# A second score buffer, values eight slots later, and the weight scales spread over the first 20 slots

## The chip, the cores and the metric

The kernel runs on one core of a Trainium2 chip. The metric is the time of one execution on the device, in microseconds (us). The kernel before takes 847.64 us, the median of three runs (847.51 to 848.23).

## What is computed

The reference is one block of a transformer on x of 4 x 2048 x 256 in fp32: attention with one head of 256, then a gated feed-forward that mixes each row with the row before it, each with a layer norm before and behind it and a residual around it.

```
x = x + layernorm(attn(layernorm(x)))
    qkv = the columns 0:64 and 192:256 of x in fp16, 64:192 in fp32, times weight_qkv
    s = softmax((q / 16) k^T);  y = s v;  attn = y out_w^T + out_b
x = x + layernorm(ffn(layernorm(x)))
    xr = mu_r x + (1 - mu_r) x_prev;  xk = mu_k x + (1 - mu_k) x_prev
    ffn = sigmoid(xr W_r^T) * (relu(xk W_k^T)^2 W_v^T)
```

## The kernel before

The 4 x 2048 rows are cut into 32 steps of 256 rows (two tiles of 128; `RT` = 2, `H` = 32), and each step's keys into four blocks of 512. A step has so eight **units**, a tile against a block. Time is counted in **slots**: slot k computes the scores of unit k, and every other stage of a step h stands at slot 8h plus an offset from a table of numbers. All engines run through the same slots, each with its own list of what it does in one; nothing else sets the order. Within a step the stages are: scores (TensorE, 5 matmuls of 512 columns into one of three PSUM banks S), a copy to the fp32 buffer `probs` with the running maximum (VectorE, `score_out`), `row_bias` behind the last block of a tile, the exponential (ScalarE, `exponents`, in place in `probs`), its upper fp16 half `p_hi` (ScalarE, `probs_high`) and the rest `p_lo` (VectorE, `probs_low`), four transposing DMAs from SyncE's queue, the values (TensorE, `attend`, 10 matmuls of 256 columns in each of eight slots), the projection, the norms and the feed-forward (`project_out`, `attention`, `turn_mix_in`, `mix`, `receptance`, `mix_keys`, `feed`, `gated`, and small norms on GpSimd). fp32 products are made of fp16 halves, three or five matmuls to a product.

In a step's first 16 slots stand `EXP` (4, 8), `HIGH` (6, 9), `LOWER` (7, 10), `TURN_P` (7, 11) for its two tiles, and `VALUES` 15: the scores of step h are in slots 8h to 8h+7, its values in 8h+15 to 8h+22. `probs` has one set of two tiles, so that the first copy of a tile waits for `p_lo` of the same tile one step earlier (line 792). The first step takes its units in another order (tile by tile in turn) and has its own offsets, `FIRST_EXP` and the like.

Ahead of the slots the kernel folds the query and key weights into one matrix, norms the first 2048 rows, splits them into fp16 halves (`planes_high` on ScalarE, `planes_low` on VectorE) and turns them by DMA. The other weights are scaled by powers taken from their peaks: `turn_weight` and `multiply_weights` in slot 2, `peaks_of` in 4, a turn of the peaks in 6, `diagonal_of_peaks` in 8, its spread and `tops` in 9, `scales` on GpSimd, `weight_high` in 11 and 13, `weight_low` in 12 and 14. The rows of batches 1 to 3 are prepared in the slots of the batch before, by four groups of stages from `PREP` on, 12 slots apart.

## Time and profile before

| | |
|---|---|
| median of three runs | 847.64 us |
| the profiled execution | 845.67 us |
| its span, first to last instruction | 843.9 us |
| TensorE busy | 796.9 us, 94% of the span |
| VectorE busy | 704.0 us, 83% |
| ScalarE busy | 516.9 us, 61% |
| GpSimd busy | 420.9 us, 50% |
| DMA | 101.59 MB, mean 120 GB/s |

The page of the profile cuts the span into 40 slices of 21.1 us and gives the busy share of an engine in each in tenths. TensorE's line is 4779999999999999999999999999999999999953: it is busy all through but for the first four slices and the last two. The chain that ended last stands for 87% of the span on TensorE and 7% on VectorE. A matmul's busy time runs from its issue to its modelled end, so that matmuls behind each other overlap; the distance between their starts is the rate.

### The profile page before, as it was taken

To read this page: it belongs to the slowest core of one execution; us is meant where nothing else is said; L and a number is where in the kernel's file an instruction comes from. 1 tells how busy PE (TensorE), PEld (TensorE's weight loads), DVE (VectorE), ACT (ScalarE), POOL (GpSimd) and SP (SyncE) were. 2 spreads that over 40 slices of the span, in tenths; PEclk is the share of its full clock that TensorE was granted. 3 is DMA by queue.
4 is the path that set the end of the run, shared out by engine and by line. 5 is a ranking of instruction groups with operands and counts; after the bars stand their busy time and mean duration, and the time that the engine had idled before them with its cause. 6 is when DMAs were issued, how large, how long until landed. Compare 5 with 4: busy or idle time off the path is not lost.

```text
span 843.9 us, 16183 instructions
## 1 busy us (share of the span) xinstructions
PE 796.9 (94%) x5873; PEld 582.2 (69%) x5873; DVE 704.0 (83%) x1808; ACT 516.9 (61%) x639; POOL 420.9 (50%) x651
## 2 busy tenths in 40 slices
PE   4779999999999999999999999999999999999953
PEld 2436677777777777777777777777777777777842
DVE  5678898987998998988898998988787787888683
ACT  3266665665676766666676666666666655667542
POOL 2020255555545565555446555654456555545872
PEclk9979999999999999999999999999999999999998
DMA  7557866557556775796445767575435455554301
GB/s 180 113 124 156 158 138 132 107 126 150 123 114 107 153 143 125 120 144 143 108 113 107 169 128 142 125 126 119 97 87 119 101 125 125 117 110 106 83 12 38
DMA packets 336575, 101.59 MB, mean 120 GB/s; under 512 B 310256, under 2 KB 336240, under 8 KB 336496
## 3 DMA queue, kind: packets, MB, share of 16 engines
q1 hardware_dynamic: 336496, 100.56, 56.7%
q8 instruction: 47, 0.77, 0.4%
q14 instruction: 32, 0.26, 0.1%
HBM read 18.75 MB, written 8.39 MB: 32 GB/s over the span
## 4 chain that ended last, share of the span: by engine, by line
PE 87%; DVE 7%; POOL 2%; issue 2%; ACT 1%; DMA 1%; SPq 1%; ACTq 0%; POOLq 0%; DVEq 0%
PE S L1038 6%; PE S L1040 6%; PE S L1039 6%; PE S L1042 6%; PE S L1041 6%; PE Y L1060 6%; PE Y L1062 6%; PE Y L1063 6%; PE Y L1061 6%; PE Y L1059 6%; PE M L1006 6%; PE M L1007 6%; PE M L1008 6%; PE M L1090 2%; PE M L1022 1%
## 5 line engine op out<-in xcount | busy, mean ns | idle before, releaser
L793 DVE TENSOR_SCALAR_CACHE_REDUCE probs<-S 128x512 f32<-128x512 f32 x256 | 173.0, 679 | 78.3 <-PE S L1042 74.9
L597 ACT ACTIVATE probs<-probs,exp_bias,kappa 128x2048 f32<-128x2048 f32 x64 | 134.0, 2094 | 68.2 <-DVE exp_bias L804 68.2
L809 DVE TENSOR_TENSOR p_lo<-probs,p_hi 128x2048 f16<-128x2048 f32 x64 | 162.5, 2539 | 1.9 <-ACT p_hi L547 1.9
L1059 PE MATMUL Y<-pt_hi,planes 128*128 128x256 f16 x512 | 139.7, 273 | 0.5 <-issue 0.5
L1060 PE MATMUL Y<-pt_lo,planes 128*128 128x256 f16 x512 | 139.7, 273 | 0.0
L1061 PE MATMUL Y<-pt_hi,planes 128*128 128x256 f16 x512 | 139.7, 273 | 0.0
L1063 PE MATMUL Y<-pt_hi,planes 128*128 128x256 f16 x512 | 139.7, 273 | 0.0
L1062 PE MATMUL Y<-pt_lo,planes 128*128 128x256 f16 x512 | 139.7, 273 | 0.0
L547 ACT ACTIVATE p_hi<-probs 128x2048 f16<-128x2048 f32 x64 | 121.9, 1905 | 1.1
L1038 PE MATMUL S<-turned,q_hi 128*128 128x512 f16 x256 | 98.7, 386 | 3.1 <-DVE q_lo L784 3.1
L615 ACT ACTIVATE att<-att,ashift,arstd 128x256 f32<-128x256 f32 x62 | 33.9, 593 | 107.4 <-POOL ashift L455 107.4
L1040 PE MATMUL S<-turned,q_hi 128*128 128x512 f16 x256 | 98.7, 386 | 0.0
L1039 PE MATMUL S<-turned,q_lo 128*128 128x512 f16 x256 | 98.6, 385 | 0.0
L1041 PE MATMUL S<-turned,q_hi 128*128 128x512 f16 x256 | 98.5, 385 | 0.0
L1042 PE MATMUL S<-turned,q_lo 128*128 128x512 f16 x256 | 98.5, 385 | 0.0
L510 POOL TENSOR_TENSOR sq_lo<-square,sq_hi 128x512 f16<-128x512 f32 x31 | 40.1, 1293 | 113.4 <-ACT sq_hi L649 113.4
L505 POOL TENSOR_TENSOR xm_lo<-mixed,xm_hi 128x512 f16<-128x512 f32 x62 | 70.7, 1162 | 33.9 <-ACT xm_hi L547 33.9
L467 POOL TENSOR_TENSOR gvar<-gmv,gate_eps 128x2 f32<-128x2 f32 x32 | 8.0, 251 | 149.3 <-DVE gmv L878 149.3
L860 DVE SCALAR_TENSOR_TENSOR mixed<-diff,mu,xt 128x256 f32<-128x256 f32 x128 | 78.2, 654 | 0.0
L625 ACT ACTIVATE xt<-M,mix_scale 128x512 f32<-128x512 f32 x32 | 22.0, 688 | 86.4 <-PE M L1090 86.4
L1059 PEld LDWEIGHTS Y<-pt_hi,planes 128*128 128x128 f16 x512 | 50.0, 98 | 32.3 <-issue 0.7
L1060 PEld LDWEIGHTS Y<-pt_lo,planes 128*128 128x128 f16 x512 | 50.0, 98 | 31.6
(179 smaller groups left out, 1941.0 us busy)
## 6 DMA issues: line engine op xcount, KB each, us to landing
x_res<-in_L_attn_x SPq DMA_DIRECT2D x32, 256.0 KB, 3.7
out_x<-gate SPq DMA_DIRECT2D x32, 256.0 KB, 3.1
xs<-in_L_attn_x SPq DMA_DIRECT2D x28, 128.0 KB, 3.3
xs<-in_L_attn_x SPq DMA_DIRECT2D x14, 256.0 KB, 4.1
pt_hi<-p_hi SPq DMA_TRANSPOSE x64, 4.5
pt_lo<-p_lo SPq DMA_TRANSPOSE x64, 3.7
pt_hi<-in_L_attn_weight_qkv SPq DMA_DIRECT2D x3, 128.0 KB, 3.1
pt_hi<-in_L_attn_weight_qkv SPq DMA_DIRECT2D x1, 256.0 KB, 3.2
```

The costliest lines, as they stand in the source:

```text
L793: dve.tensor_scalar(probs[:, t, c * BLK:(c + 1) * BLK], S[k % RING][:, :], 1.0, None, ALU.mult, ALU.max, accum_out=chunk_max[:, t, c:c + 1 ...
L809: dve.tensor_tensor(p_lo[:, t, :], probs[:, t, :], p_hi[:, t, :], ALU.subtract).then_inc(p_lo_made, 1)
L1038: pe.matmul(to, q_hi[:, h % 2, 0, rows], low, start=True, stop=False)
L1039: pe.matmul(to, q_lo[:, h % 2, 0, rows], low, start=False, stop=False)
L1040: pe.matmul(to, q_hi[:, h % 2, 1, rows], high, start=False, stop=False)
L1041: pe.matmul(to, q_hi[:, h % 2, 1, rows], rest, start=False, stop=False)
L1042: pe.matmul(to, q_lo[:, h % 2, 1, rows], high, start=False, stop=True).then_inc(s_done, 1)
L1059: pe.matmul(to[:, 0, :], low, p_h, start=first, stop=False, skip_group_check=True)
L1060: pe.matmul(to[:, 0, :], low, p_l, start=False, stop=final, skip_group_check=True)
L1061: pe.matmul(to[:, 1, :], high, p_h, start=False, stop=False, skip_group_check=True)
L1062: pe.matmul(to[:, 1, :], high, p_l, start=False, stop=False, skip_group_check=True)
L1063: mm = pe.matmul(to[:, 1, :], rest, p_h, start=False, stop=final, skip_group_check=True)
```

## The change

The buffer `probs` gets a second set (`[P, 2, RT, N]`, by the parity of the step), and the first copy of a tile waits for `p_lo` of two steps before. The offsets of `HIGH`, `LOWER`, `TURN_P` move by four to eight slots, and every stage from `INVERT` and `VALUES` on by exactly eight: values now stand 23 slots behind their scores instead of 15, and the program has eight slots more (`SLOTS` follows `STORE`, 63 for 55). The work on the weights, which stood in slots 2 to 14, is spread over slots 3 to 20, two of its turns go ahead of the first queries, and three of the four first `planes_low` go from VectorE to GpSimd. `PREP` goes from 10 to 18. The peaks are turned into bank Y[0] instead of M[0].

```
-    HIGH = (6, 9)
-    LOWER = (7, 10)
+    HIGH = (10, 13)
+    LOWER = (11, 14)
-    FIRST_LOWER = (7, 10)
-    TURN_P = (7, 11)
-    INVERT = 10
-    VALUES = 15
+    FIRST_LOWER = (10, 13)
+    TURN_P = (15, 18)
+    INVERT = 18
+    VALUES = 23
...
-    STORE = 55
+    STORE = 63
...
-    PREP, PREP_EVERY = 10, 12
+    PREP, PREP_EVERY = 18, 12
+    FOLD_AT, WEIGHTS_AT, VAL_AT, PEAKS_AT, PEAKS_TURN_AT, DIAGONAL_AT, SPREAD_AT, TOPS_AT = 3, 5, 6, 8, 11, 12, 15, 16
+    W_HIGH_AT, W_LOW_AT = (17, 19), (18, 20)
...
-        probs = sb("probs", [P, 2, N])
+        probs = sb("probs", [P, 2, RT, N])
...
             turn_planes(2)
+            turn_planes(3)
             sp.dma_start(bias_row[:, :], ...)
...
-            turn_planes(3)
...
-            for n in range(NJ):
-                pre_rsqrt(n)
+            def planes_low(n):
+                pool.wait_ge(plane_hi_made, n + 1)
+                pool.tensor_tensor(planes[:, 0, n * NT:(n + 1) * NT, 2, :], rows_of(n)[:, :, P:D],
+                                   planes[:, 0, n * NT:(n + 1) * NT, 1, :], ALU.subtract).then_inc(plane_lo_made, 1)
+            pre_rsqrt(0)
+            pre_rsqrt(1)
+            pre_rsqrt(2)
+            planes_low(1)
+            pre_rsqrt(3)
+            planes_low(2)
+            planes_low(3)
...
             def score_out(k):
...
-                if c == 0 and h >= 1:
-                    dve.wait_ge(p_lo_made, (h - 1) * RT + t + 1)
-                dve.tensor_scalar(probs[:, t, c * BLK:(c + 1) * BLK], S[k % RING][:, :], ...
+                if c == 0 and h >= 2:
+                    dve.wait_ge(p_lo_made, (h - 2) * RT + t + 1)
+                dve.tensor_scalar(probs[:, h % 2, t, c * BLK:(c + 1) * BLK], S[k % RING][:, :], ...
...
-            planes_low(1)
             pre_stats_of(3)
-            query_low(0)
             pre_norm(2)
             pre_moments_of(3)
-            planes_low(2)
+            query_low(0)
             pre_norm(3)
-            score_out(0)
-            planes_low(3)
             dve.wait_ge(kappa_made, 2)
-            score_out(1)
-            dve.wait_ge(vec_in, (1 + 2 * HALVES) * 16)
...
                     if h == 0:
-                        pe.wait_ge(val_kept, 1)
+                        pe.wait_ge(top_made, 1)
...
+            pe.wait_ge(w_rounded, 2)
+            turn_weight(2)
+            turn_weight(3)
             pe.wait_ge(qk_lo_made, 1)
             queries(0)
```

The rows below are VectorE's order at the start of the second step's scores, in the kernel before (`probs<-S` is a copy of scores, `max_copy` and `exp_bias` are `row_bias`, `peak_of`, `peak_diag` and `top` belong to the weight scales).

```order
L793 TENSOR_SCALAR probs,chunk_max<-S 128x512 [waits s_done]
L801 TENSOR_SCALAR max_copy,row_max<-chunk_max 128x4 [waits s_copied]
L804 TENSOR_SCALAR exp_bias<-row_max,minus_kappa 128x1 [waits max_made]
L809 TENSOR_TENSOR p_lo<-probs,p_hi 128x2048 [waits p_hi_made]
L793 TENSOR_SCALAR probs,chunk_max<-S 128x512 [waits p_lo_made,s_done]
L767 TENSOR_REDUCE peak_of<-M 7x1 [waits peaks_turned]
L769 TENSOR_SCALAR peak_diag<-ident,peak_of 7x7 [waits peak_kept]
L793 TENSOR_SCALAR probs,chunk_max<-S 128x512 [waits s_done]
```

The second block's copy waits there for `p_lo` of the first step. The same place in the changed kernel, from the end of the first step's copies:

```order
L815 TENSOR_SCALAR max_copy,row_max<-chunk_max 128x4 [waits s_copied]
L818 TENSOR_SCALAR exp_bias<-row_max,minus_kappa 128x1 [waits max_made]
L807 TENSOR_SCALAR probs,chunk_max<-S 128x512 [waits s_done]
L771 TENSOR_REDUCE peaks<-pt_lo 128x3 [waits vec_in,w_in]
L773 TENSOR_REDUCE peaks<-mu 128x1
L776 TENSOR_REDUCE peaks<-M 128x1 [waits out_multiplied]
L807 TENSOR_SCALAR probs,chunk_max<-S 128x512 [waits s_done] x2
L823 TENSOR_TENSOR p_lo<-probs,p_hi 128x2048 [waits p_hi_made]
L807 TENSOR_SCALAR probs,chunk_max<-S 128x512 [waits s_done]
```

Three copies of the second step now stand ahead of the first `p_lo`, and none of them waits for it. The other place is VectorE in the middle of the program, from the copy of slot 8h+5 to the normed rows `att<-res` that TensorE turns next. Before:

```order
L793 TENSOR_SCALAR probs,chunk_max<-S 128x512
L860 SCALAR_TENSOR_TENSOR mixed<-diff,mu,xt 128x256 x2
L784 SCALAR_TENSOR_TENSOR q_lo<-M,q_hi 128x512
L793 TENSOR_SCALAR probs,chunk_max<-S 128x512 x2
L801 TENSOR_SCALAR max_copy,row_max<-chunk_max 128x4
L804 TENSOR_SCALAR exp_bias<-row_max,minus_kappa 128x1
L813 SCALAR_TENSOR_TENSOR y_lo<-Y,y_hi 128x512
L809 TENSOR_TENSOR p_lo<-probs,p_hi 128x2048
L868 SCALAR_TENSOR_TENSOR gate<-rec,M 128x512
L852 TENSOR_SCALAR att<-res,rmv,rrstd 128x256 x2
```

And in the changed kernel:

```order
L807 TENSOR_SCALAR probs,chunk_max<-S 128x512
L874 SCALAR_TENSOR_TENSOR mixed<-diff,mu,xt 128x256 x2
L798 SCALAR_TENSOR_TENSOR q_lo<-M,q_hi 128x512
L807 TENSOR_SCALAR probs,chunk_max<-S 128x512
L823 TENSOR_TENSOR p_lo<-probs,p_hi 128x2048
L807 TENSOR_SCALAR probs,chunk_max<-S 128x512
L815 TENSOR_SCALAR max_copy,row_max<-chunk_max 128x4
L818 TENSOR_SCALAR exp_bias<-row_max,minus_kappa 128x1
L827 SCALAR_TENSOR_TENSOR y_lo<-Y,y_hi 128x512
L882 SCALAR_TENSOR_TENSOR gate<-rec,M 128x512
L866 TENSOR_SCALAR att<-res,rmv,rrstd 128x256 x2
```

A `p_lo` has moved from behind `y_lo` to ahead of it; the step's other `p_lo` has moved from slot 8h+2 to slot 8h+3, ahead of the `mixed` of slot 8h+4.

## Rows read from the trace of the kernel before

**Rows 1.** Windows of the whole program: us, PE, PEld, DVE, ACT, POOL busy (instructions), granted clock, DMA.
```profile
22.50:63.50 41.00, 32.93 (x141) 16.70 (x141) 28.17 (x81) 20.07 (x26) 7.08 (x17) 0.88 0.53 119
63.50:770.50 707.00, 706.98 (x5304) 519.76 (x5305) 615.65 (x1575) 456.99 (x554) 366.17 (x548) 1.00 0.60 125
770.50:843.90 73.40, 48.39 (x402) 39.80 (x400) 47.35 (x108) 32.75 (x52) 42.99 (x70) 0.93 0.24 62
```
**Rows 2.** Timeline of TensorE, start of the scores: start, us, instruction, [idle before <- releaser].
```profile
22.55 0.61 PE L1038 MATMUL S<-turned,q_hi 128*128 128x512 f16 x1 [1.61 <-DVE q_lo L784]
...
28.58 0.27 PE L1018 MATMUL M<-turned,qk_hi 128*128 128x256 f16 x1
...
34.59 0.38 PE L1038 MATMUL S<-turned,q_hi 128*128 128x512 f16 x1
...
50.05 0.59 PE L1181 MATMUL M<-peak_diag,twos 7*128 7x7 f32 x2 [3.53 <-DVE peak_diag L769]
...
63.52 0.39 PE L1038 MATMUL S<-turned,q_hi 128*128 128x512 f16 x1 [1.46 <-DVE q_lo L784]
```
**Rows 3.** Windows of two stretches in the first 60 us.
```profile
41.00:46.50 5.50, 5.17 (x16) 1.93 (x16) 2.32 (x12) 4.20 (x4) 0.00 (x0) 0.69 0.00 0
50.00:56.00 6.00, 5.95 (x21) 3.24 (x22) 4.33 (x11) 1.36 (x3) 4.32 (x12) 0.54 0.78 174
```
**Rows 4.** Groups of VectorE, 22.5 to 63.6 us: busy us, mean ns | idle before.
```profile
L793 DVE TENSOR_SCALAR_CACHE_REDUCE probs<-S 128x512 f32<-128x512 f32 x15 | 10.3, 684 | 8.9 <-PE S L1042 6.4 <-DMA mu<-in_L_ffn_mu_k 2.4
L809 DVE TENSOR_TENSOR p_lo<-probs,p_hi 128x2048 f16<-128x2048 f32 x2 | 4.6, 2289 | 1.9 <-ACT p_hi L547 1.9
L757 DVE TENSOR_REDUCE peaks<-pt_lo 128x3 f32<-128x1536 f32 x1 | 1.7, 1747 | 0.0
L705 DVE BATCH_NORM_STATS2 pst<-xs 128x6 f32<-128x256 f32 x4 | 1.4, 407 | 0.0
...
L751 DVE SCALAR_TENSOR_TENSOR wt_lo<-Y,weight_scale_of,wt_hi 128x512 f16<-128x512 f32 x1 | 0.7, 749 | 0.0
...
L804 DVE TENSOR_SCALAR exp_bias<-row_max,minus_kappa 128x1 f32<-128x1 f32 x3 | 0.6, 214 | 0.1
```
**Rows 5.** Groups of ScalarE, 22.5 to 63.6 us.
```profile
L597 ACT ACTIVATE probs<-probs,exp_bias,kappa 128x2048 f32<-128x2048 f32 x3 | 6.3, 2089 | 9.1 <-DVE exp_bias L804 9.1
L547 ACT ACTIVATE p_hi<-probs 128x2048 f16<-128x2048 f32 x3 | 5.7, 1905 | 0.1
```
**Rows 6.** Window of one step in the middle.
```profile
448.55:472.68 24.13, 24.13 (x183) 17.83 (x182) 21.93 (x61) 15.04 (x19) 13.51 (x21) 1.00 0.58 136
```
**Rows 7.** Timeline of VectorE in that step.
```profile
451.14 0.69 DVE L793 TENSOR_SCALAR_CACHE_REDUCE probs<-S 128x512 f32<-128x512 f32 x1 [1.02 <-PE S L1042]
...
459.97 0.68 DVE L813 SCALAR_TENSOR_TENSOR y_lo<-Y,y_hi 128x512 f16<-128x512 f32 x1
460.56 2.28 DVE L809 TENSOR_TENSOR p_lo<-probs,p_hi 128x2048 f16<-128x2048 f32 x1
...
463.36 0.73 DVE L852 TENSOR_SCALAR att<-res,rmv,rrstd 128x256 f32<-128x256 f32 x2
```
**Rows 8.** Timeline of TensorE in that step: first matmul of the projection, the turn behind it.
```profile
464.19 0.27 PE L1006 MATMUL M<-wt_hi,y_hi 128*128 128x256 f16 x1
...
465.50 0.60 PE L1090 MATMUL M<-ident,att 128*128 128x128 f32 x4
```
**Rows 9.** The tiles p_lo and mixed: ns min/median/max, first and last start.
```profile
L809 DVE TENSOR_TENSOR p_lo<-probs,p_hi x64: 2280/2306/3141, 46.4 to 778.9; 128x2048 f16<-128x2048 f32 x64
...
L505 POOL TENSOR_TENSOR xm_lo<-mixed,xm_hi x62: 1153/1158/1363, 121.8 to 816.0; 128x512 f16<-128x512 f32 x62
```
**Rows 10.** Timelines of VectorE and TensorE behind the last scores.
```profile
774.78 0.67 DVE L868 SCALAR_TENSOR_TENSOR gate<-rec,M 128x512 f32<-128x512 f32 x1
...
785.38 0.27 PE L1059 MATMUL Y<-pt_hi,planes 128*128 128x256 f16 x1 [0.49 <-issue]
...
789.18 0.67 DVE L868 SCALAR_TENSOR_TENSOR gate<-rec,M 128x512 f32<-128x512 f32 x1
```

More of the change, by code:

```diff
@@ L48, in sandwich @@
     EXP = (4, 8)
-    HIGH = (6, 9)
-    LOWER = (7, 10)
+    HIGH = (10, 13)
+    LOWER = (11, 14)
     FIRST_EXP = (7, 8)
     FIRST_HIGH = (7, 9)
-    FIRST_LOWER = (7, 10)
-    TURN_P = (7, 11)
-    INVERT = 10
-    VALUES = 15
-    LOAD_RES = 17
-    Y_HIGH = 23
-    Y_LOW = 23
-    PROJECT = 25
-    ATTEND = 25
-    ATT_RSQRT = 26
-    ATT_NORM = 26
-    RESIDUAL = 27
-    RES_STATS = 28
-    RES_RSQRT = 31
-    MIX_IN = 31
-    TURN = 33
-    XT = 33
-    DIFF = 33
-    MIX = (36, 37)
-    SPLIT = 39
-    SPLIT_LOW = 39
-    RECEPT = 42
-    KEYS = 42
-    RECEPT_OUT = 45
-    SQUARE = 44
-    SQUARE_LOW = 44
-    FEED = 47
-    GATE = 47
-    GATE_STATS = 48
-    GATE_RSQRT = 48
-    GATE_NORM = 49
-    FINISH = 50
-    STORE = 55
+    FIRST_LOWER = (10, 13)
+    TURN_P = (15, 18)
+    INVERT = 18
+    VALUES = 23
+    LOAD_RES = 25
+    Y_HIGH = 31
+    Y_LOW = 31
+    PROJECT = 33
+    ATTEND = 33
+    ATT_RSQRT = 34
+    ATT_NORM = 34
+    RESIDUAL = 35
+    RES_STATS = 36
+    RES_RSQRT = 39
+    MIX_IN = 39
+    TURN = 41
+    XT = 41
+    DIFF = 41
+    MIX = (44, 45)
+    SPLIT = 47
+    SPLIT_LOW = 47
+    RECEPT = 50
+    KEYS = 50
+    RECEPT_OUT = 53
+    SQUARE = 52
+    SQUARE_LOW = 52
+    FEED = 55
+    GATE = 55
+    GATE_STATS = 56
+    GATE_RSQRT = 56
+    GATE_NORM = 57
+    FINISH = 58
+    STORE = 63
     QUERY = -6
@@ L596, in exponents @@
                     act.wait_ge(att_made, (h - 3) * RT)
-                act.activation(probs[:, t, :], probs[:, t, :], ACT.Exp, bias=exp_bias[:, t:t + 1],
+                act.activation(probs[:, h % 2, t, :], probs[:, h % 2, t, :], ACT.Exp, bias=exp_bias[:, t:t + 1],
                                scale=kappa[:, 0:1], accum_out=row_sum[:, h % 4, t:t + 1]).then_inc(exp_made, 1)
@@ L603, in probs_high @@
                     act.wait_ge(pt_in[t], 32 * h)
-                copy(p_hi[:, t, :], probs[:, t, :]).then_inc(p_hi_made, 1)
+                copy(p_hi[:, t, :], probs[:, h % 2, t, :]).then_inc(p_hi_made, 1)
             def attended_high(h):
@@ L691, in _ @@
                     planes_high(n)
-                if k == 3:
+                if k == VAL_AT:
                     row_norms_of()
                     keep_val()
-                if k in (11, 13):
-                    weight_high(k - 11)
-                    weight_high(k - 10)
+                for i in range(2):
+                    if k == W_HIGH_AT[i]:
+                        weight_high(2 * i)
+                        weight_high(2 * i + 1)
         @block.vector
@@ L808, in probs_low @@
                 dve.wait_ge(p_hi_made, h * RT + t + 1)
-                dve.tensor_tensor(p_lo[:, t, :], probs[:, t, :], p_hi[:, t, :], ALU.subtract).then_inc(p_lo_made, 1)
+                dve.tensor_tensor(p_lo[:, t, :], probs[:, h % 2, t, :], p_hi[:, t, :], ALU.subtract).then_inc(p_lo_made, 1)
             def attended_low(h):
@@ L992, in _ @@
                     planes_low(n)
-                if k == 4:
+                if k == PEAKS_AT:
                     peaks_of()
-                if k == 8:
+                if k == DIAGONAL_AT:
                     diagonal_of_peaks()
-                if k == 9:
+                if k == TOPS_AT:
                     tops()
-                if k in (12, 14):
-                    weight_low(k - 12)
-                    weight_low(k - 11)
+                for i in range(2):
+                    if k == W_LOW_AT[i]:
+                        weight_low(2 * i)
+                        weight_low(2 * i + 1)
         @block.tensor
@@ L1173, in _ @@
                         turn_weight(i)
-                if k == 6:
+                if k == PEAKS_TURN_AT:
                     pe.wait_ge(peaks_made, 3)
                     pe.wait_ge(row_norms, HALVES)
-                    pe.wait_ge(q_lo_made, begun(k, QUERY))
-                    pe.transpose(PEAK_BANK[0:PEAKS, 0:P], peaks[:, :], ident[:, :]).then_inc(peaks_turned, 1)
-                if k == 9:
+                    pe.wait_ge(val_kept, 1)
+                    pe.transpose(PEAKS_BANK[0:PEAKS, 0:P], peaks[:, :], ident[:, :]).then_inc(peaks_turned, 1)
+                if k == SPREAD_AT:
                     pe.wait_ge(diag_made, 1)
-                    pe.matmul(PEAK_BANK[:, 0:PEAKS], twos[0:PEAKS, :], peak_diag[:, :], start=True,
+                    pe.matmul(PEAKS_BANK[:, 0:PEAKS], twos[0:PEAKS, :], peak_diag[:, :], start=True,
                               stop=True).then_inc(peaks_spread, 1)
```

27 lines of the change are left out of this document (12 added, 15 removed).

## The prediction

> **What bounds the kernel now.** I read the busy shares by stretch first. From 63.5 to 770.5 us TensorE is busy 706.98 of 707 us at full granted clock; in the 41 us ahead of that it works 32.9, and in the 73.4 us behind it 48.4 [rows 1]. So all idle time that a new order could win lies at the two ends, and the middle can only lose. One step in the middle takes 24.13 us, all of it TensorE, with VectorE busy 21.9 of them [rows 6]. Twelve matmuls of 256 columns stand 1.31 us apart in all, 0.109 each [rows 8]; a step has 138 of these, 40 of 512 columns at 0.217 and four small turns: 15.0 + 8.7 + 0.4 = 24.1, the step's length. The scores of eight slots are 8.7 of that, the ten query matmuls 1.1, everything else 14.3.
>
> The Trainium skill speaks against this reading: Perfetto Trace Analysis, Identifying the Most-Contended Engine, says that a matmul engine's busy share is no measure of how near it is to its limit, and that the share of weight loading is to be taken, which is 17.8 of 24.1 us here, 74%. By that rule a late input in the middle would be hidden and the term for the middle below would be nothing, the sum 3.9 us. The distance between starts bears the rule out in its warning, but leaves no room here: it is the same 0.109 us throughout, so I price a wait there in full.
>
> Next the start. TensorE's first scores start at 22.55 us and the scores of slot 16, from which on it never stops, at 63.52, after a wait for `q_lo` [rows 2]. In between VectorE waited 6.4 us for scores, 2.4 for a small DMA and 1.9 for ScalarE [rows 4], and ScalarE 9.1 us for `exp_bias` [rows 5]: with one `probs` set the chain copy, exponential 2.09, `p_hi` 1.91, `p_lo` 2.29 runs one tile at a time, and the next step's copies stand behind it. TensorE's granted clock fell to 0.69 and 0.54 of full in two stretches [rows 3], the second behind a wait of 3.53 us for `peak_diag` [rows 2].
>
> **The start, worked out.** With two sets the second and third step's scores run on during the first step's exponentials, and VectorE becomes the limit. TensorE comes to the end of slot 8's scores at about 40.0 us: slots 0 to 2 end at 28.6 as before [rows 2], plus 0.5 for two weight turns ahead of the first queries and for `q_lo` behind a norm; the queries, turns and the fold between slots 2 and 3, which took 6.0 us [rows 2], less the two moved turns (four small matmuls each, 0.9) and a wait for their copies that now goes (0.7), are 4.4; six scores at 5 x 0.217 are 6.5. From there VectorE's own list, slot 8 to slot 21's `q_lo`, is what counts. A 512-column copy takes 0.68 and the next instruction starts some 0.08 before its end, as `p_lo` 0.59 behind the start of `y_lo` [rows 7], so I take 0.61: 14 copies 8.5; three `p_lo` at 2.2, 6.6; the peaks 1.75 and a second reduction like a copy, 2.4; statistics of the next batch's rows 1.4 and their four small sums, 1.8; their norm, four instructions like those, 1.3; four `wt_lo` at 0.67, 2.7; two `q_lo` 1.2; 14 small ones at 0.21, 2.9 [rows 4]. Together 27.4 us. ScalarE, with four exponentials and three `p_hi` in the same time, 14.1 us [rows 5], and four small weight copies, is hidden. TensorE runs at most three banks ahead: while VectorE is in the second `p_lo` and the `q_lo` behind it, TensorE stands some 2.4 us, two thirds of the wait ahead of the second fall [rows 2, 3], and I let its next scores come late by 1.2 us, an estimate from one slot's scores at half rate, 2.2 instead of 1.1. So slot 24's scores start at 40.0 + 27.4 + 1.2 = 68.6, after `q_lo` of slot 21. In the kernel before slot 16 stood at the same point at 63.5; the changed kernel has by then done eight slots of scores and one set of queries more, 8.7 + 1.1 = 9.8. Gain: 63.5 + 9.8 - 68.6 = **4.7 us**. Bounds: 5.9 if the clock holds, 2.3 if it falls at all three `p_lo` (2 x 1.2 more).
>
> What else moves there costs nothing by this list: three `planes_low` on GpSimd (its instruction of that form takes 1.16 us [rows 9] against VectorE's 0.69 by the copy's rate), since it is nearly idle, 7.1 of 41 us [rows 1], and the rows that they turn are needed first by slots 2, 4 and 6; the wait for the small DMA that stood ahead of slot 2's copy now stands in slot 8, when it has long landed; the chain of the weight scales ends in slot 16, and the first to wait for it are the values of slot 23. If that cover were gone (GpSimd late by the 0.5 us of its three longer instructions each), 1.5 us.
>
> **The middle.** All offsets behind `VALUES` move by eight, so TensorE's order in a step is the same; only the two `p_lo` and `p_hi` change places. ScalarE's two `p_hi` fall into time in which it waits (it is busy 15.0 of 24.1 us [rows 6]). On VectorE one `p_lo` leaves slot 8h+2, the longest of TensorE's, and goes ahead of the copy of slot 8h+4: of its 2.2 us the idle wait of 1.02 there [rows 7] hides most of half, so all behind it is 1.1 later. The other goes from behind `y_lo` to ahead of it: 2.2 more if nothing meets it, 3.1 at the longest seen [rows 9]. Queued behind it are `y_lo`, the gate and the rows `att<-res`; TensorE waits for the first with the projection and for the last with the turn. In the step shown, where the statistics of the next batch fall into slot 8h+6, `y_lo` ends at 460.6 and is then done at 463.9 to 464.8, against the projection at 464.19; `att<-res` ends at 464.0, is done by 465.1 to 466.0, against 465.50 [rows 7, 8]. The waits are no sum, one hides the other: 0 to 0.6 us, and I take 0.3. Two steps of eight are so in each of three batches, six in all: **1.8 us lost**. Where the norm falls into slot 8h+4, six more steps, the same working ends some 0.1 us ahead of TensorE, and in the others a microsecond. Bounds: 0, and 7.2 (6 x 0.9 and 6 x 0.3) if `p_lo` always takes its longest and the semaphores add 0.3.
>
> The transposes of a step now go out together behind the values that free their buffer, in slot 8h+15 to 18, and have 15 us until slot 8h+23: no price.
>
> **The end.** One more round of eight slots without scores. Its TensorE work, 14.3 us, is not new but comes out of the middle. A round took 14.4 from gate to gate [rows 10], so a bare extra round costs 0.1. Both `p_lo` of the last step now fall into it, the second ahead of `y_lo`: 2.2 to 3.1 on VectorE, of which TensorE's lead in such a round takes the larger part; against it the wait of 0.49 for the last step's transposes [rows 10] goes. Between a gain of 0.5 and a loss of 2.6 I take **0.8 lost**, nearer to the first.
>
> **Sum.** 4.7 - 1.8 - 0.8 = 2.1 us. The profiled execution took 845.67, 1.8 more than its span of 843.9: the span becomes 841.8, that execution 843.6. The median of the runs shown lies 2.0 above the profiled one, so I forecast **845.5 us**.
>
> **Rivals.**
> - The middle is free. `p_lo` meets nothing on GpSimd in slot 8h+6, and every input is there in time. For it: 2.306 is the median of `p_lo` [rows 9], and by 2.2 us the working above ends ahead of TensorE. Against: ScalarE hands `xm_hi` to GpSimd just then. Then 4.7 - 0.8 = 3.9 us are gained: 843.7 us.
> - The start gives nothing. TensorE falls to half rate at each `p_lo`, three times 1.2: the gain is 2.3, and the middle and the end take 2.6. For it: the clock fell twice in this stretch [rows 3]. Against: most gaps are now shorter. 847.9 us.
> - Slower: the second `p_lo` waits in every step with work for the next batch until GpSimd's `xm_lo` of 1.16 us is through. Then `y_lo` is 0.3 later still than the longest above: 0.9 us in six steps, 0.4 in six more, 7.8 us, against 4.7 - 0.8: 3.9 lost, 851.5 us. It decides from 0.33 us on in each of the twelve. For it: `p_lo` goes up to 3.14 us in the trace; against: a `p_lo` that starts in the middle of an `xm_lo` waits for its rest only.
>
> On the last: the Trainium skill, SBUF — State Buffer, Who interferes with whom, says that a VectorE instruction with two SBUF inputs and a GpSimd one that reads SBUF share an exclusive port, and that the one issued later stands until the other is through. By that rule the wait is up to one whole `xm_lo`; the longest `p_lo`, 0.86 over its shortest, agrees [rows 9].
>
> **How the numbers follow.** The forecast has 0.45 (own range 843.9 to 847.1), the free middle 0.22, the start that gives nothing 0.18, the slower one 0.15. Below 0.2%, 1.7 us, a measurement of this kernel can't tell a change. Faster: 0.28 + 0.22 + 0.03 = 0.53. Same: 0.16 of the forecast, 0.12, 0.02, together 0.30. Slower: 0.01 + 0.03 + 0.13 = 0.17. The range, 842.0 to 850.0, takes in the free middle and half of the slower case.
>
> **What would show it.** In the changed profile slot 24's scores, the second behind which values stand, near 68.6 us, and VectorE without a gap from 40 to 68 but for one near 54; TensorE's clock down once, near 53. Waits of the projection's first matmul for `y_lo`, or of the turn for `att<-res`, between 100 and 740 us, six of 0.3 each. Some 88 to 89 us from the last scores to the end of the span, where 73.4 are now [rows 1]. It is wrong if TensorE shows no wait in the middle, if the scores of slot 24 start more than 2 us from 68.6, or if TensorE waits for transposes.

## The result, and the profile after

| | before | after | ratio, 95% interval |
|---|---|---|---|
| first comparison, medians | 847.58 us (4 runs, 846.97 to 848.23) | 841.85 us (4 runs, 841.49 to 843.48) | 0.9946 [0.9927, 0.9966] |
| second comparison, medians | 846.35 us (35 runs, 843.91 to 848.95) | 842.62 us (12 runs, 841.53 to 846.63) | 0.9968 [0.995, 0.9985] |
| profiled execution (span) | 845.67 us (843.9) | 843.48 us (841.7) | |

The change makes the kernel faster: the medians differ by 5.7 us in the first comparison and by 3.7 in the second (by the ratios 4.6 and 2.7). Between the two profiled executions it is 2.2 us. That last number is what the prediction's sum was made for, 2.1; the medians say more, and where the difference comes from is the main subject below. One execution, the profiled one of old_places, took 1064.86 us at a granted clock of 0.745 of full and is left out everywhere.

The changed kernel's windows, in the columns of [rows 1], cut at slot 24's scores and at the end of the last scores:

```profile
22.50:69.20 46.70, 40.09 (x184) 20.00 (x184) 36.81 (x101) 26.53 (x29) 7.34 (x19) 0.87 0.60 130
69.20:752.50 683.30, 683.12 (x5120) 502.08 (x5121) 564.03 (x1524) 437.44 (x533) 366.03 (x528) 1.00 0.60 124
752.50:841.70 89.20, 64.55 (x536) 53.61 (x534) 56.90 (x133) 41.36 (x66) 57.14 (x89) 0.88 0.37 81
```

TensorE is busy 683.12 of 683.30 us in the middle, again full. So a difference can only lie in three numbers: where the middle begins, how long it is, how long the rest is. They stand for every profile of this study in one table, in us: A is the start of the first scores from which TensorE hardly stops (slot 16 with the values at 15, the first four rows; slot 24 with the values at 23, the others), B the time from there to the start of the last score matmul, C from there to the end of the span. To set a kernel of the first kind beside one of the second, add 9.8 to its A, take 24.13 from its B and add 14.35 to its C: with the later values eight slots' scores and one set of queries more stand ahead of A, one step less in B, and a round without scores more in C, as the prediction counted.

| profile of | A | B | C | span |
|---|---|---|---|---|
| before | 63.52 | 706.38 | 74.0 | 843.9 |
| before_again | 61.88 | 706.37 | 74.2 | 842.5 |
| buffer_only | 63.24 | 706.37 | 74.2 | 843.8 |
| before_warm | 62.85 | 706.37 | 71.6 | 840.8 |
| after | 69.19 | 682.93 | 89.6 | 841.7 |
| after_again | 67.93 | 682.59 | 89.2 | 839.7 |
| weights_early | 69.75 | 682.60 | 89.3 | 841.6 |
| old_places_again | 66.76 | 682.24 | 95.8 | 844.8 |
| keep_warm | 64.72 | 683.76 | 91.8 | 840.3 |
| light_start | 65.51 | 686.17 | 92.4 | 844.1 |
| warm_both | 64.81 | 683.86 | 86.5 | 835.2 |
| warm_old_places | 62.85 | 682.24 | 90.4 | 835.5 |
| combined | 61.81 | 682.60 | 86.5 | 830.9 |

From before to after: A 63.52 + 9.8 - 69.19 = 4.1 gained, B 682.93 - (706.38 - 24.13) = 0.7 lost, C 89.6 - (74.0 + 14.35) = 1.2 lost, together 2.2.

TensorE at the start of the changed kernel, columns as in [rows 2]:

```profile
23.32 0.61 PE L1047 MATMUL S<-turned,q_hi 128*128 128x512 f16 x1 [2.66 <-DVE q_lo L798]
...
52.15 0.39 PE L1047 MATMUL S<-turned,q_hi 128*128 128x512 f16 x1 [2.26 <-DVE q_lo L798]
...
53.19 0.63 PE L1051 MATMUL S<-turned,q_lo 128*128 128x512 f16 x1
...
65.37 0.39 PE L1047 MATMUL S<-turned,q_hi 128*128 128x512 f16 x1 [2.00 <-DVE probs L807]
...
69.19 0.61 PE L1047 MATMUL S<-turned,q_hi 128*128 128x512 f16 x1 [0.43 <-DVE q_lo L798]
```

The wait for `peak_diag` is gone; two waits of 2.26 and 2.00 us are left, each about the length of a `p_lo` on VectorE, and behind each the matmuls go at half rate for a stretch (0.63 in place of 0.38 for one of 512 columns): the granted clock falls from 2.4 to 1.2 GHz. Windows of the two stretches, against [rows 3]:

```profile
50.00:55.00 5.00, 2.85 (x9) 1.12 (x10) 4.75 (x14) 1.21 (x1) 0.09 (x1) 0.78 0.90 201
66.00:70.00 4.00, 3.57 (x16) 1.80 (x15) 4.00 (x10) 1.58 (x2) 0.00 (x0) 0.57 0.58 132
```

VectorE is busy 4.75 of 5 and 4.00 of 4 us there: it sets the pace, as forecast. The first scores, too, run at half rate (0.61 for one). This is read from the matmuls: the granted clock in the windows can miss it, and in the kernel before it stands at 1.00 from 20 to 30 us, where the first scores take 0.61 to 0.64 each [rows 2].

The place in a step on which the term for the middle rested, in the changed kernel: VectorE in a step whose slot 8h+6 has the statistics of the next batch, then the projection's first matmul on TensorE, against [rows 7] and [rows 8].

```profile
461.63 1.17 DVE L874 SCALAR_TENSOR_TENSOR mixed<-diff,mu,xt 128x256 f32<-128x256 f32 x2
...
463.93 2.28 DVE L823 TENSOR_TENSOR p_lo<-probs,p_hi 128x2048 f16<-128x2048 f32 x1
466.13 1.39 DVE L718 BATCH_NORM_STATS2 pst<-xs 128x6 f32<-128x256 f32 x4
...
469.00 0.68 DVE L827 SCALAR_TENSOR_TENSOR y_lo<-Y,y_hi 128x512 f16<-128x512 f32 x1
```

```profile
470.55 0.27 PE L1015 MATMUL M<-wt_hi,y_hi 128*128 128x256 f16 x1
```

`y_lo` ends at 469.68 and is needed at 470.55: no wait, 0.87 us to spare. In the whole middle TensorE waits once:

```profile
132.65 0.28 PE L1015 MATMUL M<-wt_hi,y_hi 128*128 128x256 f16 x1 [0.18 <-DVE y_lo L827]
```

`p_lo` and GpSimd's `xm_lo` by the groups of the whole program (busy us, mean ns, idle before), against [rows 9]:

```profile
L823 DVE TENSOR_TENSOR p_lo<-probs,p_hi 128x2048 f16<-128x2048 f32 x64 | 149.8, 2341 | 2.0 <-ACT p_hi L559 2.0
...
L874 DVE SCALAR_TENSOR_TENSOR mixed<-diff,mu,xt 128x256 f32<-128x256 f32 x128 | 62.1, 528 | 0.0
```

```profile
L507 POOL TENSOR_TENSOR xm_lo<-mixed,xm_hi 128x512 f16<-128x512 f32 x62 | 125.7, 2046 | 29.1 <-ACT xm_hi L559 29.1
```

In the kernel before the same groups had means of 2539, 654 and 1162 ns. VectorE's two became shorter, GpSimd's longer.

And the end, TensorE's longest waits behind the last scores, against [rows 10]:

```profile
808.22 0.40 PE L1015 MATMUL M<-wt_hi,sq_hi 128*128 128x256 f16 x1 [3.67 <-POOL sq_lo L512]
813.92 1.11 PE L1099 MATMUL M<-ident,att 128*128 128x128 f32 x4 [2.96 <-DVE att L866]
822.23 0.28 PE L1015 MATMUL M<-wt_hi,sq_hi 128*128 128x256 f16 x1 [3.35 <-POOL sq_lo L512]
...
830.90 0.28 PE L1015 MATMUL M<-wt_hi,sq_hi 128*128 128x256 f16 x1 [3.42 <-DVE sq_lo L917]
```

No transposes are waited for there any more.

### The profile page after: what moved, and what is told of

Read it like the earlier page. It is cut to its first block, busy times and chain, and to the rows that moved or that the text cites. A ratio compares the mean times of both kernels' runs of the same rounds, so it can differ in the third digit from the quotient of the medians.

```text
span 841.7 us, 16181 instructions
## 1 busy us (share of the span) xinstructions
PE 797.7 (95%) x5873; PEld 582.9 (69%) x5873; DVE 671.4 (80%) x1805; ACT 514.2 (61%) x639; POOL 436.3 (52%) x654
## 4 chain that ended last, share of the span: by engine, by line
PE 85%; DVE 9%; issue 2%; POOL 1%; ACT 1%; DMA 1%; SPq 0%; ACTq 0%; POOLq 0%; DVEq 0%
PE S L1047 6%; PE M L1015 6%; PE S L1048 6%; PE S L1051 6%; PE S L1049 6%; PE S L1050 6%; PE Y L1068 6%; PE Y L1072 6%; PE Y L1071 6%; PE Y L1070 6%; PE M L1017 6%; PE Y L1069 6%; PE M L1016 6%; PE M L1099 2%; DVE p_lo L823 1%
## 5 line engine op out<-in xcount | busy, mean ns | idle before, releaser
L823 DVE TENSOR_TENSOR p_lo<-probs,p_hi 128x2048 f16<-128x2048 f32 x64 | 149.8, 2341 | 2.0 <-ACT p_hi L559 2.0
L507 POOL TENSOR_TENSOR xm_lo<-mixed,xm_hi 128x512 f16<-128x512 f32 x62 | 125.7, 2046 | 29.1 <-ACT xm_hi L559 29.1
L512 POOL TENSOR_TENSOR sq_lo<-square,sq_hi 128x512 f16<-128x512 f32 x31 | 43.2, 1392 | 144.6 <-ACT sq_hi L661 144.6
L1068 PEld LDWEIGHTS Y<-pt_hi,planes 128*128 128x128 f16 x512 | 50.1, 98 | 30.7
L874 DVE SCALAR_TENSOR_TENSOR mixed<-diff,mu,xt 128x256 f32<-128x256 f32 x128 | 62.1, 528 | 0.0
L1070 PEld LDWEIGHTS Y<-pt_hi,planes 128*128 128x128 f16 x512 | 50.2, 98 | 5.9
```

The source lines that it names most:

```text
L823: dve.tensor_tensor(p_lo[:, t, :], probs[:, h % 2, t, :], p_hi[:, t, :], ALU.subtract).then_inc(p_lo_made, 1)
L1068: pe.matmul(to[:, 0, :], low, p_h, start=first, stop=False, skip_group_check=True)
L1070: pe.matmul(to[:, 1, :], high, p_h, start=False, stop=False, skip_group_check=True)
```

## The experiments

**The same two kernels again.** The question was why the medians give 5.7 us where the profiles give 2.2. No edit.

> The kernel before, unchanged, profiled a second time. The two first profiles differ by 2.2 us of span (843.9 to 841.7), the medians by 5.7. Theory A: executions of one kernel differ by some 2 us at their start, where TensorE's clock falls or holds; the first profile of the kernel before was an early one of its kind. Then this profile has scores of slot 16 at 64.5 to 66 us instead of 63.5, and the same 780.4 us (707 + 73.4) from there to the end within 0.5. Theory B (rival): the executions differ in the middle or at the end, and slot 16 stands at 63.5 again within 0.5.

> The changed kernel, unchanged, profiled a second time; its first profile was the slowest of four executions (843.5 against 841.5 to 842.0). Theory A (the start varies): slot 24's scores at 67 to 68 us instead of 69.2, span near 840, and 772.5 us from there to the end within 0.5. Theory B (the middle or the end varies): slot 24 at 69.2 again, and the two microseconds behind it. Time 841.5 to 842.2.

Measured: before_again 846.33 us (10 runs, 843.78 to 848.43), after_again 842.62. In before_again the scores of slot 16 start here:

```profile
61.88 0.39 PE L1038 MATMUL S<-turned,q_hi 128*128 128x512 f16 x1 [1.45 <-DVE q_lo L784]
```

1.64 us earlier than in the first profile; B is the same to 0.01 us. Slot 24's scores in after_again start at 67.93, 1.26 earlier than in after; the other 0.7 of its 2.0 us lie behind (0.3 in B, 0.4 in C), which theory A had not. So these two pairs of executions differ for the most part ahead of slot 16 or 24, as theory A had it (64.5 to 66 was the wrong direction for before_again, since this execution was one of the shorter ones). Single executions of one kernel spread over 5 us: one profile of each can't give the gain.

**One part alone: the second buffer; and the weights back where they were.**

```
 buffer_only: before, with
-        probs = sb("probs", [P, 2, N])
+        probs = sb("probs", [P, 2, RT, N])
 (and its five uses as in the change; all offsets as before)
 weights_early: after, with
-    FOLD_AT, ... TOPS_AT = 3, 5, 6, 8, 11, 12, 15, 16
-    W_HIGH_AT, W_LOW_AT = (17, 19), (18, 20)
+    FOLD_AT, ... TOPS_AT = 2, 2, 3, 4, 6, 8, 9, 9
+    W_HIGH_AT, W_LOW_AT = (11, 13), (12, 14)
```

> One part alone: the kernel before with the second probs set and its wait for p_lo of two steps before, all offsets as they were. My theory: the chain of exponential, p_hi and p_lo stays in slots 7 to 11 ahead of the copies on VectorE, so that the first step's p_lo still stands ahead of copies in program order, and the set by itself gains little: 846 to 848. Rival: the wait for p_lo was the stall, and the buffer alone gives most of the gain: 842 to 844.

> One part undone: the changed kernel with the work on the weight scales back in slots 2 to 14. My theory: the start is bound by VectorE's list, which keeps the same instructions in another order, so nothing much is lost: 0 to 1.5 us slower than the changed kernel, from waits of TensorE for peak_diag in slot 9 as in the kernel before. Rival: the spreading is half of the gain, 844 to 846.

buffer_only: 846.2 us, ratio to before 0.9997 [0.9982, 1.0011]: the set alone gains nothing. weights_early: 843.54, 0.9978 [0.9962, 0.9994], 0.9 above after_again, and A at 69.75 instead of 69.19 and 67.93; the wait for `peak_diag` is back with 0.83 us, and one of 3.94 for `q_lo` stands ahead of slot 16's scores. The spread of the weights adds little of the gain, and with intervals of 0.002 to each side the 0.9 itself is not certain.

What is left of the edit is more than the second set and the later values, and the start of slot 8's scores tells where the gain arises:

```profile
43.12 0.64 PE L1038 MATMUL S<-turned,q_hi 128*128 128x512 f16 x1
```

```profile
38.85 0.38 PE L1047 MATMUL S<-turned,q_hi 128*128 128x512 f16 x1
```

They start at 43.12 us in the kernel before and at 38.85 in the changed one (43.05 and 37.79 in the second pair, 43.05 in buffer_only, 40.19 in weights_early). The copy of slot 8 is the first that writes the second set, so the 4.3 us (2.9 in weights_early, whose work on the weights stands where it did) are there before that set is in use. From slot 8's scores to A the changed kernel then takes 30.3 us, the kernel before 20.4 and the 9.8 of the table, 30.2. Gone ahead of slot 8 are two waits of TensorE in the kernel before:

```profile
31.45 2.00 PE L1129 MATMUL M<-res 128*128 128x256 f32 x8 [0.74 <-ACT res L547]
...
41.33 0.27 PE L1178 MATMUL M<-ident,peaks 128*7 128x128 f32 x1 [2.26 <-DVE q_lo L784]
```

The first was for a copy of the turned weights, which now go ahead of the first queries, the second for `q_lo`, since the peaks were turned into the queries' bank. No run takes back these two or the `planes_low` on GpSimd by themselves, so what each is worth stays open, and it is not shown that the second set with the later values gains anything at the start. The later `p_lo` can't be had without the second set: with one set the copy of slot 8 would wait for a `p_lo` that stands behind it in VectorE's own list.

**`p_hi`, `p_lo` and the transposes in their old places within a step.**

```
-    HIGH = (10, 13)
-    LOWER = (11, 14)
-    TURN_P = (15, 18)
+    HIGH = (14, 17)
+    LOWER = (15, 18)
+    TURN_P = (15, 19)
```

> The changed kernel with p_hi in slots 14 and 17, p_lo in 15 and 18 and the transposes in 15 and 19, which are the kernel before's places within a step (6, 9, 7, 10, 7, 11) eight slots on; the start keeps its order. My prediction priced the other places at 1.8 us lost in the middle; the trace shows one wait of 0.18 us there. Theory 'the move is free for TensorE, because the new p_lo is the shorter one': no difference in time, median within 1 us of the changed kernel's 842.6 (841.5 to 843.6); p_lo's mean goes back from 2.34 to about 2.5 us, xm_lo on GpSimd from 2.05 to about 1.2, VectorE's busy time from 671 to about 700 us, and TensorE's stretch from slot 24's scores to the last ones stays at 682 to 683. Rival 'the move cost what I priced': it is 1 to 2 us faster, 840.6 to 841.6, and the stretch behind slot 24 is that much shorter. Rival 'the move is what gains': 844 or more, with waits of TensorE for y_lo or att in the middle.

> The kernel of old_places once more, whose profile was of a disturbed execution; its timed runs fell into two groups, 841.1 to 841.5 (2) and 845.4 to 847.5 (9). Theory 'a late p_lo makes TensorE wait': waits for y_lo or att in the middle, together 2 us or more, or a stretch behind the last scores 2 us or more longer than 89.4. Rival 'the start and the clock in it': no wait above 0.3 us between slot 24's scores and the last ones, and slot 24's scores 2 us or more later than 69.2. Rival 'the clock at the end': a span behind the last scores of 91 us and more, with the granted clock below 0.8 of full over 20 us of it, in executions of the slower group alone. xm_lo's mean is nearer to 1.2 than to 2.05 us in either case, p_lo's nearer to 2.5.

The profile used is that of old_places_again. The times: 845.75 (11 runs), then 845.74 us (12 runs, 841.0 to 846.93), some 3 above the change's median. By the ratios to the kernel before (0.9978 and 0.9988, where the change had 0.9968) it is 0.8 to 1.7 us, with intervals that overlap. The times fall into two groups, 841.0 to 841.5 (4 of 23) and 845.0 to 847.5 (19), where 13 of the change's 16 lie below 843.5. So "free" was wrong as a whole, but it holds for the middle: B is 682.24, with not one wait in it. After's 682.93 is 0.69 longer: 0.34 by the one wait for `y_lo` (0.18 of idle time, but 0.45 us between two starts that are 0.11 apart elsewhere), and 0.34 because its first two score matmuls behind A still go at half rate. So the move of `p_lo` costs the middle 0.34 us. Two groups of old_places_again, VectorE's and GpSimd's, show that the durations go back with the order:

```profile
L823 DVE TENSOR_TENSOR p_lo<-probs,p_hi 128x2048 f16<-128x2048 f32 x64 | 163.2, 2550 | 0.0
```

```profile
L507 POOL TENSOR_TENSOR xm_lo<-mixed,xm_hi 128x512 f16<-128x512 f32 x62 | 72.8, 1195 | 33.8 <-ACT xm_hi L559 33.8
```

What it loses, it loses at the end, C 95.8 for 89.6: TensorE waits for transposes twice, and for `att`, and later runs at half clock from 810 to 820 us (0.63 there in the changed kernel). The profile is of an execution of the longer group.

```profile
764.50 0.27 PE L1068 MATMUL Y<-pt_hi,planes 128*128 128x256 f16 x1 [0.52 <-issue]
...
773.29 0.66 PE L1099 MATMUL M<-ident,att 128*128 128x128 f32 x4 [1.97 <-DVE att L866]
```

```profile
810.00:820.00 10.00, 5.87 (x29) 4.15 (x28) 8.55 (x19) 3.04 (x5) 6.54 (x10) 0.51 0.00 0
```

**The clock: work for TensorE in its waits.** keep_warm adds matmuls whose results nothing reads.

```
+            def warm(to, count):
+                for _ in range(count):
+                    pe.matmul(to[:, :], qk_hi[:, 0, 0:P], turned[:, 0, 0:NT, 0, :], start=True, stop=True)
 scores(k), ahead of its waits:
+                if k == 0:  warm(S[2], 6)
+                if k == 16: pe.wait_ge(s_copied, k - RING + 1); warm(S[k % RING], 8)
+                if k == 23: pe.wait_ge(top_made, 1); warm(Y[0], 7)
 (and the wait for s_copied further down is left out for k == 16)
```

> The changed kernel with idle work for TensorE: matmuls of 512 columns whose results nothing reads, six ahead of slot 0's scores, eight ahead of slot 16's and seven ahead of slot 23's, where TensorE now waits 2.7 to 2.9, 2.26 and 2.00 us. Theory 'the executions differ, and the changed kernel loses, because the clock falls in or behind these waits': it stays at full from 30 to 75 us, slot 24's scores start near 67 (67.9 and 69.2 in the two traces), the median is 840 to 841.5 and the executions spread over 1 to 2 us, where the changed kernel's spread over 5. Rival 'the clock falls whatever TensorE does there, or VectorE's list alone sets slot 24': median 842 to 843.5, the spread as before, and slot 24 between 67.9 and 69.2.

Measured 842.15 us (6 runs, 839.95 to 842.53). The granted clock is 1.00 in each 5 us from 30 to 75 us, and A comes to 64.72, 3.2 to 4.5 earlier than with the clock falling, more than expected; none of the six took longer than 842.53, and their spread is 2.6 us. But the median is in the rival's range: of this profile's gain, one wait of 0.99 us for `y_lo` at 88.69 us and 2 us and more at the end (C 91.8) take most. So the start's clock is shown to matter, and the end has its own:

```profile
800.00:830.00 30.00, 14.40 (x87) 10.15 (x85) 16.27 (x34) 13.52 (x23) 14.75 (x24) 0.77 0.08 27
```

**Both ends.** warm_both is keep_warm with nine such matmuls ahead of the last turn and twelve ahead of the last three gates' matmuls (`turn_mix_in` for h = 31, `feed` for h from 29 on).

> keep_warm, and the same kind of idle work behind the last scores: nine matmuls of 512 columns ahead of the last turn and twelve ahead of the last three gates' matmuls, where TensorE waits 2.96, 3.67, 3.35 and 3.43 us. Without them the stretch from the last scores to the end was 89.2 (after_again), 89.6 (after), 91.8 (keep_warm) and 92.4 us (light_start), the longer ones with a granted clock of 0.5 to 0.8 between 800 and 830 us. Theory 'the clock falls in these waits and costs up to 3 us': the stretch becomes 86 to 88.5 us, the median 838 to 840, the spread under 1.5 us. Rival 'the chain of the last steps runs over VectorE and GpSimd, TensorE's clock does not matter there': 89 to 92 us, median 841.5 to 842.5.

837.12 us (5 runs, 836.99 to 837.35), ratio 0.9894 [0.9875, 0.9912] to before, 0.9 below what was expected. C is 86.5, the clock in the same window 1.00, and the spread of 5 us is down to 0.4:

```profile
800.00:830.00 30.00, 21.32 (x144) 13.43 (x141) 17.65 (x40) 13.48 (x23) 15.41 (x27) 1.00 0.08 27
```

So the clock's falls in the waits at the two ends make the spread between executions of the changed kernel, and cost it 5 to 6 us in the median.

**The change, and its `p_lo`, with the clock held.** before_warm has idle matmuls in the waits of the kernel before (six ahead of slot 0's scores, eight in slot 6, twelve in slot 9, five in slot 16, the end as above). warm_old_places is warm_both with the offsets of old_places.

> The kernel before with the idle work of warm_both where this one waits: six matmuls of 512 columns ahead of slot 0's scores, eight ahead of the turn of the peaks in slot 6, twelve ahead of their spread in slot 9, five ahead of slot 16's scores, and at the end nine and three times twelve as in warm_both. With the clock held in both, the pair before_warm and warm_both (837.1) measures the change without what the clock adds or takes. Theory 'the change gains by its order, about what the prediction's terms say with the clock held (start 5.9, middle 1.1 for the wait at 88.87 us, end 1.0)': slot 16's scores at 60.5 to 61.5, median 840 to 841.5, 3 to 4.4 above warm_both. Rival 'the gain was the clock's, the order gives nothing': 836.5 to 838. In either case a spread under 1.5 us.

> warm_both with p_hi and p_lo in their old places within a step (14, 17; 15, 18; transposes 15, 19). old_places_again lost nothing in the middle but took 95.8 us from the start of its last score matmul to the end, where the changed kernel took 89.6 and 89.2; its waits there were 20.9 us together against 17.0, and its clock half from 810 to 820 us. Theory 'the late transposes and p_lo lengthen the chain at the end': 1.5 to 4 us slower than warm_both, 838.6 to 841, with the waits of 0.5 us for transposes and of 2 us for att still there. Rival 'it was the clock at the end': within 0.7 us of 837.1.

before_warm: 843.11 us (12 runs, 841.62 to 844.3, a spread of 2.7 where under 1.5 was expected), 6.0 above warm_both (5.8 by the ratios to the kernel before, 0.9963 and 0.9894). It is more than expected because the clock was not held throughout: in slot 9 the twelve matmuls fill half of the wait, and it still falls in the rest.

```profile
48.90 0.59 PE L1200 MATMUL M<-peak_diag,twos 7*128 7x7 f32 x2 [2.63 <-DVE peak_diag L769]
```

```profile
50.00:55.00 5.00, 5.00 (x19) 2.48 (x17) 3.48 (x8) 1.10 (x3) 4.42 (x12) 0.50 0.65 143
```

What that costs is read from VectorE, which waits for these scores once and from there to slot 16 not again:

```profile
51.77 0.69 DVE L793 TENSOR_SCALAR_CACHE_REDUCE probs<-S 128x512 f32<-128x512 f32 x1 [1.45 <-PE S L1051]
```

At most 1.45 us are the clock's, then, and 0.5 those of the idle matmuls themselves: slot 16's scores start 1.23 us behind the start of their `q_lo`, 0.75 in the kernel before. Some 4 us are left for the change, an estimate, so that it gains without the clock's falls too: even at 841.2 us before_warm would lie above the rival's 838. By the table the pair of profiles gives A 62.85 + 9.8 - 64.81 = 7.8 gained, B 1.6 lost, C 0.6 lost: 5.6, and the spans differ by 840.8 - 835.2 = 5.6. Of the 7.8, 5.2 are there when slot 8's scores start (41.36 against 36.13).

warm_old_places: 837.44 us, 0.3 above warm_both. The time is the rival's, but not for its reason: the end is 3.9 us longer (90.4 for 86.5) though the clock is held, with the waits for transposes of 1.18 and 0.76 us and 1.97 for `att` that the first theory named. It is made up for because A is 2.0 earlier, and B 1.6 shorter, since no `y_lo` waits for a `p_lo`. The order of `p_lo` within a step moves time from one end to the other. The 3 us between the medians of old_places and the changed kernel are 0.3 with the clock held in both, so they are mostly the clock's.

**Less on VectorE at the start.**

```
-    PREP, PREP_EVERY = 18, 12
-    W_HIGH_AT, W_LOW_AT = (17, 19), (18, 20)
+    PREP, PREP_EVERY = 26, 10
+    W_HIGH_AT, W_LOW_AT = (24, 26), (26, 28)
 and exp_bias with a place for each parity of step
```

> The changed kernel with less of VectorE's work ahead of slot 24: the next batch's rows begin in slot 26 and follow every 10 slots (before: 18, every 12), the weights are split in slots 24 to 28 (before: 17 to 20), and exp_bias has a place for each parity of step. By my list of VectorE's work, the limit between 40 and 68 us, this takes out four wt_lo at 0.67, the statistics and sums at 1.8 and the norm at 1.3: 5.8 us. Theory 'VectorE's list sets slot 24': its scores start 3.5 to 5.5 us earlier, at 63 to 65.5, and with the middle as it is the median is 838 to 840. Rival 'the waits of TensorE and its clock set it': slot 24 not earlier than 66.5, median 841 to 843. Rival 'given back': slot 24 earlier, but waits of 2 us or more behind it, for wt_lo or the planes of the next batch: 842 to 844.

842.29 us (10 runs, 841.44 to 845.86): A is 65.51, 2.4 to 3.7 earlier than with the full list, and given back, the third theory, though the waits are not for `wt_lo` or the planes. B is 3.2 longer than after's, by two waits like this one on TensorE:

```profile
494.24 0.28 PE L1015 MATMUL M<-wt_hi,y_hi 128*128 128x256 f16 x1 [1.68 <-DVE y_lo L827]
```

and ahead of it on GpSimd and VectorE:

```profile
487.09 4.32 POOL L507 TENSOR_TENSOR xm_lo<-mixed,xm_hi 128x512 f16<-128x512 f32 x2
487.28 3.11 DVE L823 TENSOR_TENSOR p_lo<-probs,p_hi 128x2048 f16<-128x2048 f32 x1
490.31 2.21 DVE L732 TENSOR_SCALAR xs<-xs,pmv,prstd 128x256 f32<-128x256 f32 x4
...
493.50 0.68 DVE L827 SCALAR_TENSOR_TENSOR y_lo<-Y,y_hi 128x512 f16<-128x512 f32 x1
```

A long `p_lo` of 3.11, issued 0.19 us behind an `xm_lo`, and the norm of the next batch (2.21) stand between the last `q_lo` and `y_lo`. That is the mechanism of the prediction's middle term, with the norm in slot 8h+6 in the place of the statistics.

**Combined.** warm_both, with light_start's later weights and `exp_bias`, and `PREP, PREP_EVERY = 26, 8`, which puts the batch's statistics into slot 8h+2 and its norm into 8h+4 of each step.

> warm_both with the later weights and the doubled exp_bias of light_start, but the next batch's rows in slots 26, 34, 42 and 50, so that in each of these steps the statistics stand in slot 8h+2 and the norm in 8h+4 and none stands ahead of y_lo in 8h+6 or 8h+7. light_start lost two waits of 1.7 us for y_lo in the middle, where its third block of rows has its statistics in 8h+6 and its second its norm there. Theory 'the place of the batch work decides the waits in the middle': no wait for y_lo above 0.3 us between 70 and 740 us, slot 24's scores at 61 to 64.7, median 835 to 838.5. Rival 'VectorE has no room in the middle for what leaves the start': waits of 2 us or more there again, median 839 or more.

832.77 us (4 runs, 832.55 to 833.23), ratio 0.9843 [0.9822, 0.9863] to before: 13.8 us faster than the kernel before and some 10 faster than the change, and below the expected 835 to 838.5. Against warm_both A is 3.0 earlier (61.81) and B 1.3 shorter (682.60), C the same (86.5); in the middle:

```profile
61.80:744.80 683.00, 682.81 (x5122) 502.03 (x5121) 570.97 (x1538) 439.23 (x538) 380.09 (x530) 1.00 0.60 125
```

TensorE is idle 0.2 of 683 us. The place of the batch work decides the waits in the middle; VectorE has the room.

## Why the prediction came out as it did

**Start: 4.7 forecast, 4.1 measured.** Number and place were right: `peak_diag`'s wait goes, and slot 8's scores end at 39.9 us in the changed profile (40.0 forecast). The reason was right in part. The prediction named the one `probs` set and its chain as what holds the start up, yet by its own numbers slot 8's scores start at 38.9 instead of 43.1, 4.2 of the 4.7 us, before the second set is in use, and so it came out; buffer_only, with the set alone, gains nothing. From there VectorE's list was counted with 27.4 us; with the clock held in keep_warm it is 64.72 - 37.15 = 27.6. The mis-sized part is the clock: one fall near 53 was priced with 1.2 us, there were two, and the same stretch took 69.19 - 39.93 = 29.3, 1.7 more than with it held. What the prediction had not seen is that slot 8 itself stands 2.8 us later than it must (39.93 against 37.15), since the first scores, behind a wait of 2.66 us, run at half rate too, as they did before [rows 2].

**Middle: 1.8 lost forecast, 0.7 measured, half of it by one wait of 0.18.** This step failed: the prediction's own sign was six waits of 0.3. In the step shown I had `y_lo` done 0.6 late to 0.3 early; it was 0.87 early. The order was as I read it, and 1.1 and 2.2 us of `p_lo` did move ahead of it. But I left the other instructions at the lengths of the old order. The second pair of `mixed` in this step took 1.17 us in the new order, and in the old one, on VectorE:

```profile
454.19 1.78 DVE L860 SCALAR_TENSOR_TENSOR mixed<-diff,mu,xt 128x256 f32<-128x256 f32 x2
```

These 0.61 us, with the 0.3 of my early end, for which `p_lo` had 2.2 us, account for the 0.87. What the pair met, old order and new, is GpSimd's `sq_lo`:

```profile
454.33 1.36 POOL L510 TENSOR_TENSOR sq_lo<-square,sq_hi 128x512 f16<-128x512 f32 x1 [3.83 <-ACT sq_hi L649]
```

```profile
460.69 1.43 POOL L512 TENSOR_TENSOR sq_lo<-square,sq_hi 128x512 f16<-128x512 f32 x1 [4.38 <-ACT sq_hi L661]
```

In the old order the second `mixed` (454.58 to 455.97) was issued 0.25 us behind its start and ended 0.28 behind its end; in the new one `sq_lo` starts 0.94 us ahead of the pair, and only its rest is in the way.

GpSimd's `xm_lo` now meets `p_lo`, and there GpSimd is the one that stands. Its pair in the old order, and the first of the pair in the new one:

```profile
457.76 2.27 POOL L505 TENSOR_TENSOR xm_lo<-mixed,xm_hi 128x512 f16<-128x512 f32 x2 [0.96 <-ACT xm_hi L547]
```

```profile
464.40 2.82 POOL L507 TENSOR_TENSOR xm_lo<-mixed,xm_hi 128x512 f16<-128x512 f32 x1 [1.04 <-ACT xm_hi L559]
```

2.82 us for one `xm_lo`, where two took 2.27, while `p_lo` took 2.28, its median. So the rival that VectorE waits a whole `xm_lo` had the collision right and, here, the loser wrong. In the whole program 28 of the 62 `xm_lo` take over 1.6 us (up to 3.27), each issued while a `p_lo` ran. But in the five steps of the middle in which the norm falls into slot 8h+4, `xm_lo` is issued 0.30 to 0.36 us first, and `p_lo` takes 2.94 to 3.01; in one of them TensorE then waits, the 0.18 at 132.65 us:

```profile
127.63 4.32 POOL L507 TENSOR_TENSOR xm_lo<-mixed,xm_hi 128x512 f16<-128x512 f32 x2 [2.78 <-ACT xm_hi L559]
```

```profile
127.99 2.95 DVE L823 TENSOR_TENSOR p_lo<-probs,p_hi 128x2048 f16<-128x2048 f32 x1
```

The Trainium skill's rule (SBUF — State Buffer, Who interferes with whom) gives both when it is read for the new order, since the one issued later stands. The trace agrees: `p_lo` is first at 463.93 us against 464.40, `xm_lo` at 127.63 against 127.99.

Where the batch's work does fall ahead of `y_lo`, or the start is early, the wait appears in full (1.68 twice in light_start, 1.09 once in warm_both), and B grows with it (686.17 and 683.86 for 682.24): each wait lengthens the distance between two starts by its idle time and some 0.16 us more. The prediction had read from the Trainium skill (Perfetto Trace Analysis, Identifying the Most-Contended Engine) that with weight loading at 74% of a step such a wait would be hidden; in this kernel it is not.

**End: 0.8 lost forecast, 1.2 measured** (0.7 between before_again and after_again), 89.2 us from the end of the last scores where 88 to 89 stood, and no wait for transposes. Nearly right in size, but half understood: some 3 us of C are clock (86.5 with it held), of which the prediction had nothing. The kernel before loses 2.4 in the same way (71.6 for 74.0 in before_warm), so that only 0.6 of the 1.2 is clock.

**Sum and median.** 2.1 forecast, 2.2 between the profiled executions. The step from there to the median failed: "the median lies 2.0 above the profiled one" was taken as a property of the kernel, and it was one of the execution. Before's profiled one was among its shorter ones (845.67, of 843.9 to 849), after's the longest of its first four. The median of 841.85 lies outside my own range of the forecast, 843.9 to 847.1, and 0.15 below the wide one; the first ratio, taken of the 847.64 us from which the forecast was made, gives 843.1, and the second median is 842.62, both inside it. That the sum agrees with the one pair of profiles to 0.1 us is luck: the second pair gives 2.7, and the terms were off by 0.6, 1.1 and 0.4, the middle's against the other two. Why the changed kernel gains more in the median than in that pair stays open; the mean granted clock of its executions (0.970 to 0.985) is not above that of the kernel before (0.978 to 0.988).

**The rivals.** "The middle is free" comes nearest, with 3.9 us and 843.7, but not for its reason: `p_lo` does meet `xm_lo`. "The start gives nothing" is out, 4.1 against its 2.3, though the clock fell twice, as it had feared. "Slower" is out with one wait in place of twelve.

## What to carry to other kernels

Cut a profile at the places where the bound engine begins and ends to run without a stop, and compare executions stretch by stretch: here that told in one table which of several microseconds belong to an edit and which to an execution. Where executions of one kernel spread by several microseconds, look at the granted clock behind each wait of TensorE at the ends, and fill those waits with idle matmuls before judging an order. When an instruction moves, price its neighbours on VectorE and GpSimd in the new order, not at the lengths of the old one.
